# Two layers on five queues: a new order for the stages of PE, ACT, DVE and POOL

## The reference

```python
h = concat(patches @ W + b, W_txt[x_txt] + positions)
# layer 0
h = h + attn0(layernorm(h))     # relu(Q K^T / 8) V, then FFN 64-128-64, layernorm
h = h + moe0(layernorm(h))      # top-1 of 8 experts, each expert takes at most C tokens
# layer 1
h = h + attn1(layernorm(h))     # 16 heads of 4: q (norm(k)^T norm(v)) / N, projection, gelu
h = h + moe1(layernorm(h))      # top-2 of 8 experts 64-256-64 with gelu
```

## Time and profile before

| what | value |
|---|---|
| three runs | 849.8, 847.78, 849.07 us, median 849.07 |
| span of the profiled execution (the page gives no other time for it) | 846.4 us |
| PE busy | 729.7 us, 86% |
| DVE busy | 612.2 us, 72% |
| ACT busy | 481.7 us, 57% |
| POOL busy | 433.1 us, 51% |
| chain that ended last | PE 26%, ACT 15%, DVE 14%, issue 9% of the span |

### The profile page before, as it was taken

The page is one execution under the profiler, slowest core; times in us unless marked ns, Lnnn a source line. Parts: engine busy times, 40 slices in busy tenths (PEclk is TensorE's granted clock), DMA queues, the critical chain, the costliest instruction groups (busy, mean ns, idle before and its releaser), DMA issues.

```text
span 846.4 us, 15831 instructions
## 1 busy us (share of the span) xinstructions
PE 729.7 (86%) x4619; PEld 487.1 (58%) x4619; DVE 612.2 (72%) x2308; ACT 481.7 (57%) x980; POOL 433.1 (51%) x470
## 2 busy tenths in 40 slices
PE   3589999999988689965789989989989999899995
PEld 1366777666655257643456555556555656566672
DVE  4557899989678536576777889888888977786231
ACT  1255655555541146642246877766788666777552
POOL 5732617773764600246646667667676763223222
PEclk8599999999997889995679999999999999999988
DMA  7910000000000023220022221222221122223200
GB/s 216 359 53 9 14 8 19 22 21 5 5 4 3 4 58 97 75 66 12 6 57 57 62 56 17 57 59 63 62 63 41 31 55 61 62 62 61 62 14 7
DMA packets 60976, 43.69 MB, mean 52 GB/s; under 512 B 29100, under 2 KB 56252, under 8 KB 60636
## 3 DMA queue, kind: packets, MB, share of 16 engines
q1 hardware_dynamic: 51820, 36.35, 17.2%
q0 software_dynamic: 7200, 4.17, 2.4%
q10 hardware_dynamic: 1872, 2.18, 0.9%
HBM read 31.66 MB, written 13.47 MB: 53 GB/s over the span
## 4 chain that ended last, share of the span: by engine, by line
PE 26%; ACT 15%; DVE 14%; issue 9%; POOL 2%; DMA 1%; DVEq 0%; ACTq 0%; POOLq 0%
ACT scratch L715 7%; PE psum L628 6%; PE psum L1140 5%; PE psum L1141 4%; ACT L715 3%; PE psum L1340 3%; ACT L664 2%; PE psum L1147 2%; DVE xt L788 1%; PE psum L1322 1%; PE psum L1118 1%; PE psum L602 1%; ACT L659 1%; DVE kh L885 1%; DVE stats L1507 1%
## 5 line engine op out<-in xcount | busy, mean ns | idle before, releaser
L715 ACT ACTIVATE scratch<-psum,fb 128x512 f32<-128x512 f32 (+2 forms) x288 | 172.2, 665 | 37.4 <-PE psum L1141 36.1
L628 PE MATMUL psum<-scratch,w_fw 128*64 128x256 f32 (+2 forms) x1152 | 141.7, 383 | 11.4 <-DVE scratch L978 5.7
L538 POOL TENSOR_TENSOR prob<-prob,scratch 128x256 f32<-128x256 f32 (+2 forms) x126 | 79.3, 629 | 141.0 <-DVE scratch L978 139.4
L497 POOL DMA_INDIRECT uu<-expert_out,slot_i x80 | 83.2, 1040 | 88.3 <-issue 68.7
L1079 POOL DMA_INDIRECT slots_buf<-xt,slot_i x80 | 82.5, 1032 | 68.0 <-DVE slot_i L1754 45.8
L628 PEld LDWEIGHTS psum<-scratch,w_fw 128*64 128x64 f32 x1152 | 79.1, 140 | 56.5 <-DVE scratch L978 13.5
L1065 POOL DMA_INDIRECT emb<-in_table,w_ids x64 | 63.4, 991 | 55.8 <-DVE stats L1507 33.5
L1405 ACT ACTIVATE prob<-psum 128x292 f32<-128x292 f32 (+1 forms) x160 | 55.1, 396 | 52.2 <-PE psum L1207 52.1
L1140 PE MATMUL psum<-kh,fw_hi 128*128 128x512 f32 x176 | 80.0, 455 | 0.6 <-ACT scratch L715 0.5
L1141 PE MATMUL psum<-kh,fw_lo 128*128 128x512 f32 x176 | 71.8, 408 | 0.0
L978 DVE SCALAR_TENSOR_TENSOR scratch<-psum,w_fb,X 128x256 f32<-128x256 f32 (+1 forms) x119 | 54.4, 460 | 16.9 <-PE psum L628 15.5
(11 more groups left out here) (272 smaller groups left out, 1715.7 us busy)
## 6 DMA issues: line engine op xcount, KB each, us to landing
X<-share_buf SPq DMA_DIRECT2D x32, 512.0 KB
slots_buf<-zeros SPq DMA_DIRECT2D x8, 352.0 KB, 4.9
expert_out<-zeros SPq DMA_DIRECT2D x8, 352.0 KB, 4.9
out<-H SPq DMA_DIRECT2D x16, 128.0 KB
X<-in_patches ACTq DMA_DIRECT2D x3, 576.0 KB, 7.3
slots_buf<-xt,slot_i POOLq DMA_INDIRECT x80, 2.2
uu<-expert_out,slot_i POOLq DMA_INDIRECT x80, 2.5
emb<-in_table,w_ids POOLq DMA_INDIRECT x64
```

The costliest lines, as they stand in the source:

```text
L497: pool.indirect_dma_start(yg[b % 2][0:rows, s, :], None, expert_out, bass.IndirectOffsetOnAxis(slot_i[0:rows, b, (s + 1) % SLOTS:(s + 1) % ...
L538: pool.tensor_tensor(total[t % 2][:, 0:z], total[t % 2][:, 0:z], part[m % PARTS][:, 0:z], ALU.add).then_inc(sem("summed"), 1)
L628: last = pe.matmul(bank(6 + n % 2)[h * D:(h + 1) * D, 0:z], w["fw2"][:, e * J + j, :], hid[(J * n + j) % (J * UNITS)][:, h * z:(h + 1) * z ...
L715: act.activation(hid[m % (J * UNITS)][:, 0:z], bank(2 + m % 4)[:, 0:z], ACT.Gelu, bias=fb1[:, e * J + j:e * J + j + 1]).then_inc(sem("gelu ...
```

## The change

All due times, all shifts and the places of the 44 fills are new. The set of stages, their instructions, buffers and transfers stay, and the function of each stage is untouched. Lines of the new kernel from the tables on are 72 higher (L715 is L787 there). Some of the lines that the prediction speaks of:

```diff
-        DVE_ONCE = ((39.1, "prep", 0), (176.25, "late_weights", 0), (715.75, "moe_gains", 0), (762.5, "low_moe", 0))
...
-        ACT_TWO = ((68.5, "roots4"), (76, "stack4"), (80, "square"), (89.25, "roots_kv"), (117.25, "gelu_proj"), (122, "roots5"),
-                   (133.25, "stack5_even"), (135.5, "stack5_odd"), (162.5, "copy_w8"))
...
+        ACT_TWO = ((58, "roots4"), (77, "stack4"), (81, "square"), (89.25, "roots_kv"), (117.25, "gelu_proj"), (123.5, "roots5"), (133,
+                   "stack5_even"), (135.5, "stack5_odd"), (164.5, "copy_w8"))
```

More of the change, by code:

```diff
@@ L259, in early_fusion_kernel @@
[L259 to L263, removed]
+        POOL_ONE = ((8.25, "gather_a"), (38.75, "gather_b"), (124.5, "offset"), (364.75, "scatter_a"), (384, "scatter_b"))
@@ new lines, in early_fusion_kernel @@
+        PE_ONE = ((93.5, "t1"), (106.5, "q"), (120, "k"), (130, "scores0"), (130.5, "v"), (136, "scores1"), (140.25, "scores2"), (145.25, "attend_a"),
+                  (146, "scores3"), (153, "attend_b"), (155.5, "scores4"), (162.5, "attend_c"), (171.5, "o_turn"), (180.75, "t2"), (194, "ffn1"),
+                  (206.5, "ffn2"), (217.25, "y_turn"), (265, "t3"), (277, "gate"), (287.25, "count"))
+        ACT_ONE = ((48.5, "roots1"), (98.5, "stack1"), (111, "q_high"), (125.25, "k_high"), (132.5, "relu0"), (139, "relu1"), (144, "relu2"), (154.25,
+                   "relu3"), (157.75, "relu4"), (168.5, "o_copy"), (188, "stack2"), (198.5, "ffn_relu"), (210, "y_copy"), (232, "root2"), (253.75,
+                   "root3"), (271, "stack3"))
@@ L264, in early_fusion_kernel @@
+        DVE_ONE = ((30.75, "norm1a"), (46.75, "norm1b"), (104.5, "q_low"), (112.25, "k_low"), (126.75, "vals"), (168, "resid"), (212.25, "norm2a"),
+                   (226.25, "norm2b"), (235, "norm3a"), (249.25, "norm3b"), (268.5, "gate"), (286.75, "place"))
         MOE, DOWN_LAG, GELU_LAG, WEIGH_LAG, SUM_LAG, BACK_LAG, FINISH_LAG = 170, 1.5, 0.75, 2.5, -0.5, 12.75, 12
         B_START, B_STEP, B_READY = -9, 2, -82
-        FILLS_A = (598.59, 618.25, 639.37, 640.99, 664.91, 671.9, 686.57, 690.06, 696.2, 700.31, 723.39, 728.2, 731.2, 733.55, 756.22, 770.26)
@@ L330, in early_fusion_kernel @@
-        DVE_TWO = ((42.25, "mixed"), (44.25, "mixed_stats"), (64.75, "norm4"), (80, "kv_b"), (81.5, "sum_squares"), (88.5, "kvnorm_inv"),
-                   (89.25, "kvnorm"), (91.5, "gram_s"), (94.5, "own_heads"), (102.75, "add_input"), (106, "fold"), (113.25, "pre_bias"),
-                   (114.75, "resid2"), (119.75, "resid2_stats"), (122, "norm5"), (129.5, "low5_even"), (131.8, "low5_odd"), (135.75, "route_logits"),
-                   (138.25, "route_first"), (145, "route_next"), (146.25, "route_second"), (147.25, "route_shares"))
+        PE_TWO = ((75, "t4"), (78.75, "kv"), (97.5, "gram"), (100, "gains_k"), (102, "by_q"), (106.25, "by_proj"), (114.5, "proj"), (130, "t5"),
+                  (135.75, "route"), (159.75, "t8"))
```

145 lines of the change are left out of this document (98 added, 47 removed), and 52 rows, old and new, of tables (ACT_MOVED, DVE_MOVED, PE_MOVED).

## The result

The new order takes 795.75 us (median of 4 runs, 793.93 to 799.24) against 848.88 for the old one (4 runs): a ratio of 0.9367 with a 95% interval of 0.9336 to 0.9398, 53 us less. The forecast was 821 and its range ended at 805. The direction was right, and half of the gain was missing from the sum.

A forecast was written before the change was run, and what follows sets the result against it. It took a loop over several queues, paced by ACT with its table loads, to bound the even part of layer 1; −19 − 4 + 2 − 3 − 4 = −28 gave a span of 818.4, plus 2.7: 821 us, range 805 to 847.

The forecast's parts named there:

- The loop: Layer 1, even part: ACT's table loads pace each batch; two fewer loads and a gelu unit cut 24.9 to about 21.0.
- The forecast for the even part: Layer 1, even part: −19 us (bounds 0 and −30), 1.4 us a batch over 13.7 batches, giving 23.5 us a batch.
- the floor under the loop: Layer 1, even part: with the loop under 22.7 us a batch, PE's own work and small waits decide.
- The waits that I kept: Layer 1, even part: PE's waits for weigh, 11.4 us, stay because DVE gets no less to do; 30.1 becomes 18.7.
- The end of layer 0: Close of layer 0: moved moe work hides under the scatters and batch 14 gets slots earlier; −3 us (−5 to +1).
- The named step: Close of layer 0: with moe_gains no longer ahead of its gate, batch 14 gets its slots 2.6 us earlier.
- The experts and the warm-up: Experts: full on PE, unchanged. Warm-up of layer 1: kv_b earlier and three up moved into idle time, −4 us (−1 to −8).
- my step: Warm-up of layer 1: kv_b of batch 0 now stands ahead of mixed of batch 1 and its statistics; 1 to 2.5 us.
- The first `gram`: Sign in the new profile: the first gram of layer 1 loses most of its 7.8 us wait.
- Layer 0, even part: Layer 0, 60 to 240 us: some new bank waits, worst in WIDE, and some old waits gone; +2 us (−4 to +25).
- The start: Start of layer 0: q_low of batch 0 no longer waits behind norm1a of batch 2; −4 us (−6 to 0).
- The tail: End of the span: t8 of batch 15 and its copy some 6 us later, still just in time; 0 (0 to +3).

The follow-up runs named there:

- e15: Old kernel with only roots4 moved beside the other roots from batch 4 on, batch 15 left in place: 831.36 us, ratio 0.9791.
- e9: New kernel with the single shifts of up (units 34 to 110, even part of layer 1) taken out: 813.37 us, ratio 0.9566.
- e10: New kernel with gram, gains_k, by_q and by_proj of batches 4 to 13 at their old due times: 812.91 us, ratio 0.9552.
- e2: Layer 0 in the new order, everything behind it in the old: 829.98 us, ratio 0.9829 to the old kernel.
- e5: Old kernel with only moe_bias, moe_gains and low_moe moved behind the last count and place: 847.87 us, ratio 0.9974.
- e7: New kernel with moe_bias, moe_gains and low_moe back ahead of the last gates and place: 799.11 us, ratio 0.9414 to the old kernel.
- e1: Layer 0 in the old order, everything behind it in the new: 813.23 us, ratio 0.9605 to the old kernel.
- e6: Old kernel with only the start changed (q_low, k_low, k_high and t1 of the first batches moved): 844.65 us, ratio 0.9968.
- e13: Kernel of e9 plus nine constant matmuls, three ahead of gram of each of batches 7, 10 and 12: 820.17 us, ratio 0.9649.
- e8: New kernel without its 44 fills (132 matmuls whose result nobody reads): 799.26 us, ratio 0.9412 to the old kernel.

## Why the prediction was wrong, and where it was right

*The loop, right, and its price nearly.* The table loads were on the path that paced a batch. With them alone out (e15) a batch fell from 25.0 to 23.8, DVE's waits for L699 from 19.6 in 340 us to 0.2 in 212, and the time by 17.9. The forecast for the even part was 19, at 23.5 a batch. Cause and size agree here.

*The step that failed* is the floor under the loop: "PE needs 113.64/5 = 22.7 of that", and "From there on PE's own work and its small waits decide." I took PE's busy time as its work. A batch of the forecast's 23.5 us is these 22.7 and 0.8 of waits. Measured are 22.9, and they are 21.8 of busy time and 1.05 of idle time. So the whole surplus is in the busy time, and the idle time is a little longer than I had it. The even part, from `kv_b` of batch 4 on, in the old kernel, in e15 (nine batches) and in the new kernel:

```profile
464.27:739.27 275.00, 249.60 (x1563) 161.65 (x1563) 230.32 (x824) 201.11 (x341) 175.23 (x194) 0.99 0.25 53
```

```profile
464.00:676.00 212.00, 198.31 (x1279) 131.69 (x1280) 189.56 (x685) 140.04 (x261) 155.26 (x169) 1.00 0.26 56
```

```profile
439.32:690.99 251.67, 240.08 (x1566) 160.61 (x1566) 229.91 (x827) 173.35 (x319) 179.05 (x194) 1.00 0.27 58
```

PE is busy for 22.7, 22.0 and 21.8 us a batch with the same matmuls, and the loads alone bring most of the fall. Part is the clock: the earlier trace rows has a mean of 0.97 in the window from which I took the 22.7, and two of the five batches in it, that from 563.78 to 589.63 and the last one, ran at 0.93. But the nine batches at 1.00 show 22.0 to 23.0 busy as well, 22.5 in the mean. At full clock a matmul of `down` takes 386 ns before (440 to 580) and 385 after (440 to 690), but 368 of them keep PE busy for 46.3 us and 704 for 87.0, so 126 and 124 ns each: they overlap, and now follow each other more closely. What holds them apart no run isolates. The difference is 0.6 us a batch, 8 us over the 13.7 batches of my term.

*The waits that I kept* were right in their sum by luck, and wrong in kind. "I keep those for `weigh`, 5.7 + 5.7 = 11.4 [...] nothing in the change gives it less to do." The waits for `weigh` are 1.5 us now, at the same DVE work (20.9 us a batch in both). So they weren't for DVE's capacity but for the order of the stages. Others came in their place, for `gelu` above all. In e15 those for `weigh` are still there, 8.8 us in 212, and in the new kernel they are gone. Which shifts took them away stays open: with `up` back (e9) or `gram` back (e10) they stay at 1.5 and 1.4 us, and what returns is PE's wait for `kvnorm` ahead of `gram` (L635 behind L880), 8.4 and 7.9 us where the new kernel has 0.9.

*The end of layer 0* was priced at −3, for `moe_gains`. It gave 6.6 up to `b_turn`, and the experts behind it some 2.4 more (the segment from `b_turn` to `kv_b` is 80.6 before, 78.2 in e2). The named step was about right in size for the slots (3.9 in e5), and e7 puts the three stages at 4 or less. What I hadn't seen is the closing order of gates and places, 7.3 of the 10.5 us up to the last `place`, though 3.9 of the 10.5 went to fills ahead of `b_turn`; and that PE, which had stood still for 6.79 us before `b_turn`, began the experts at a mean clock of 0.78:

```profile
298.50:310.10 11.60, 10.94 (x58) 7.58 (x60) 3.24 (x7) 6.28 (x13) 0.00 (x0) 0.78 0.18 51
```

The wait was in my rows, and I let the experts' own stretch stay as "full on PE": PE was busy, but at its lower clock.

*The experts and the warm-up* had 0 and −4, and −12.5 came between the first `b_turn` and `kv_b` of batch 4. 2.4 are the clock that the end of layer 0 hands over. With the order behind layer 0 alone (e1), `b_turn` to `kv_b` 0 is 74.7 us in place of 80.6, at nearly the same busy time of PE (73.9 and 74.9). `kv_b` no longer stands 3.2 us behind the end of `kv`, as it did behind `mixed`: that was my step, at more than the 1 to 2.5 I had given it. The rest is PE's waits ahead of `kv` (0.8 and 0.6) and inside the experts (1.5 for DVE's L1766), in the stretch that I had called full; in e1 they are gone. From `kv_b` 0 to 4 the pair of profiles gives 4.9; the other profiles of either order put the order's part at some 3, and the rest is luck of this execution. Together that is over the 8 that I had put on the term at most. The first `gram` still waits 6.88 for `kvnorm`, where I had expected most of its 7.8 to go, since `mixed` now stands between `kv_b` and the sum of squares: everything came earlier, and that wait stayed.

*Layer 0, even part:* +2 was forecast, −3.2 came. PE does wait more, 9.2 us in 180 where it waited 6.8. Yet it is busy for less with more matmuls (170.76 us for 1173, 173.22 for 1154), at a clock of 1.00 in both: the same mistake as with the floor. In e6, where only the start moved, `q_low` of batch 15 gained 1.1 more than the first `scores0`.

*The start:* −4 was forecast, −2.7 came at `scores0`, and e6 measured 2.7 (1 to 5) for it alone. Over all profiles `scores0` came 3.9 us earlier in the mean, so the term was sound.

*The tail:* 0 was forecast, −3.9 came, without any idle time to win. Before, PE was busy from 814 to 821 at a mean clock of 0.62, behind and in a stretch of narrow matmuls of 36 and 72 columns; by my estimate from this row, 7.00 us at 0.62, full clock there is worth about 2.7. It is luck of the execution in part: in e2, whose order there is the old one too, the last segment is 104.3 us and not 107.1.

```profile
814.00:821.00 7.00, 7.00 (x53) 6.05 (x54) 1.29 (x6) 3.60 (x10) 1.48 (x6) 0.62 0.10 22
```

*In sum,* by the marks: the start gave 2.7 for 4, layer 0 3.2 for −2, its close 6.6 for 3, experts and warm-up 12.5 for 4, the even part with the tail 27.2 for 19; together 52.2 for 28. Of the 24 that were missing, the even part with the tail has 8, the experts and the warm-up 8.5, layer 0 five and its close 3.6; the start had 1 too much. One mistake stands behind most of them: I took PE's busy time as its work, and wrote that nothing is to be won where its row is full. A full row held time at the lower clock and matmuls that followed each other less closely than they can.

## What to carry to other kernels

In a pipeline over several in-order queues, follow the loop from one batch's stage to the same stage of the next, and price an edit by what it takes off this loop: ACT was idle for 43% of the span, and its table loads were still worth 17.9 us. Then don't take the waits that remain, nor PE's busy time, as a floor: compare busy time with the granted clock of the same window, and look at what one batch takes at full clock. Before a difference between two profiles is explained, look how far the same stretch moves between executions of one order. And judge a piece of an order inside its order: single pieces undone cost 16 to 23 us each where all together had gained 33, so neither an edit alone in the old kernel nor its removal from the new one gives its share.

## What the runs showed of the hardware

A wait of PE of 2.07 us in the middle of dense work was followed by some 7 us at 1.2 GHz (e9), and the fall of the clock cost that batch more than the wait: 3.0 us against 2.2. Not every such wait is followed by it: the one of 2.54 us in e13, with nine constant matmuls behind it, left the clock at 1.00. The clock also fell while PE was busy without a pause, with matmuls of one column (`moe_bias`, and the fills behind it at 0.54 from 274 to 278) and of 36 and 72 columns (0.62 from 814 to 821 before):

```profile
270.00:274.00 4.00, 4.00 (x29) 3.06 (x27) 0.45 (x3) 0.00 (x0) 3.09 (x4) 0.88 0.03 4
274.00:278.00 4.00, 4.00 (x16) 2.33 (x16) 2.44 (x9) 0.02 (x1) 3.09 (x4) 0.54 0.02 2
```

The Trainium skill (TensorE: Matmul & The Clock Gate, Part 1) says that a hardware monitor sets the clock by how busy PE has been; the row of e9 agrees (1.00 before the wait, 0.51 behind it), and the last two rows show the lower clock with PE busy throughout. Runs of one kernel differ in their mean clock, and the time goes with it: the 19 runs of the old kernel beside e5 to e8 go from 849.82 at 0.927 to 845.71 at 0.939, and a line through all of them falls by about 4 us for 0.01. Runs at one clock still differ by 2 us (846.54 to 848.73 at 0.933).
